# A two-layer decoder on one core: the first attention's norm, projections and value masks in four chunks, GpSimd's turn reordered, one clearing moved

## The reference

```python
def _L0_attn_ref(x, Wq, Wk, Wv, rel_table, gamma, beta):
    q, k, v = (split_heads(x @ W) for W in (Wq, Wk, Wv))   # 16 heads of 8
    attn = softmax(einsum('bhqd,bhkd->bhqk', q, k) * e ** (-0.5))
    bias = rel_table[rel_index].reshape(-1).reshape(h, s, s)
    attn = attn + bias[None]                                # after the softmax
    out = einsum('bhqk,bhkd->bhqd', attn, v)
    out = (out - mu) / sqrt(var + EPS) * gamma + beta
    return out
x = x + _L0_attn_ref(_layernorm(x), ...)
x = x + _L0_xattn_ref(_layernorm(x), ctx_1024, ...)
```

## Time and profile before

| | us |
|---|---|
| time, median of 3 runs | 1696.14 |
| lowest and highest | 1691.09, 1700.21 |
| the profiled execution | 1698.46 |
| its span | 1696.7 |

### The profile page before, as it was taken

How to read it: one execution, slowest core, us unless ns; L and a number is a source line. 1 busy time by engine, 2 the same in 40 slices (tenths; PEclk the granted TensorE clock), 3 DMA queues, 4 the chain that set the end, 5 groups by cost and what they waited for, 6 DMA issues and landing times.

```text
span 1696.7 us, 41331 instructions
## 1 busy us (share of the span) xinstructions
PE 1500.9 (88%) x17052; PEld 956.8 (56%) x17052; DVE 1102.6 (65%) x1846; ACT 868.1 (51%) x1794; POOL 779.0 (46%) x683
## 2 busy tenths in 40 slices
PE   4888999999999788867599999999999999759998
PEld 2556888865444355533366666666666666535554
DVE  5786555532342488868388888888888888515554
ACT  1332333335655333314377777777777777723332
POOL 3665121200000178857477887777777775000000
PEclk9866999989999899977799999999999999969999
DMA  5003000023211230333646556555455455023321
GB/s 114 1 2 102 3 2 3 2 67 99 62 38 24 64 77 1 65 70 73 120 120 127 123 129 129 129 124 127 124 123 129 125 124 115 8 85 76 68 58 22
DMA packets 62458, 129.58 MB, mean 76 GB/s; under 512 B 15709, under 2 KB 37982, under 8 KB 59102
## 3 DMA queue, kind: packets, MB, share of 16 engines
q1 hardware_dynamic: 62270, 126.92, 32.3%
HBM read 100.22 MB, written 26.67 MB: 75 GB/s over the span
## 4 chain that ended last, share of the span: by engine, by line
PE 62%; POOL 13%; DVE 9%; ACT 9%; issue 5%; DMA 2%; SPq 1%; ACTq 0%; DVEq 0%; POOLq 0%
PE ps L831 12%; PE ps L843 9%; POOL ARENA L1879 7%; PE ps L1675 7%; PE ps L1659 4%; POOL ARENA L1885 3%; PE ps L1622 3%; ACT ARENA L1829 3%; PE ps L1613 2%; ACT ARENA L1807 2%; PE ps L520 2%; PE ps L570 2%; PE ps L530 2%; PE ps L1636 2%; PE ps L512 2%
## 5 line engine op out<-in xcount | busy, mean ns | idle before, releaser
L1749 DVE TENSOR_REDUCE ARENA<-ps 112x2 f32<-112x1000 f32 x384 | 456.7, 1198 | 122.3 <-PE ps L1636 119.3
L1829 ACT ACTIVATE ARENA<-ps 125x448 f32<-125x448 f32 x768 | 378.4, 549 | 128.1 <-PE ps L1659 127.1
L1879 POOL TENSOR_TENSOR ARENA<-ARENA 64x500 f32<-64x500 f32 x192 | 266.8, 1390 | 106.8 <-ACT ARENA L1807 88.4
L107 POOL TENSOR_TENSOR rs<-rs,mhalf 128x1 f32<-128x1 f32 x96 | 58.1, 605 | 377.7 <-DVE rs L102 377.5
L831 PE MATMUL ps<-XT,ARENA 128*128 128x448 f32 x544 | 222.4, 553 | 0.0
L1659 PEld LDWEIGHTS ps<-ARENA 64*125 64x125 bf16 x3072 | 122.5, 134 | 134.0 <-ACT ARENA L1829 70.4
L1659 PE MATMUL ps<-ARENA 64*125 64x112 bf16 x3072 | 169.1, 229 | 19.6 <-ACT ARENA L1829 18.5
L1675 PE MATMUL ps<-ARENA 125*17 125x112 f32 x6144 | 185.6, 261 | 0.0
L831 PEld LDWEIGHTS ps<-XT,ARENA 128*128 128x128 f32 x544 | 105.6, 196 | 100.6 <-issue 100.4
L843 PE MATMUL ps<-ARENA 128*128 128x448 f32 x400 | 161.5, 539 | 0.0
L1636 PE MATMUL ps<-ARENA 64*112 64x500 bf16 x768 | 152.8, 387 | 9.0 <-DVE ARENA L1749 8.9
(11 more groups left out here) (228 smaller groups left out, 2205.9 us busy)
## 6 DMA issues: line engine op xcount, KB each, us to landing
ARENA<-key_parts SPq DMA_DIRECT2D x192, 187.5 KB, 4.2
ARENA<-in_ctxT SPq DMA_DIRECT2D x96, 250.0 KB, 3.7
key_parts<-ARENA SPq DMA_DIRECT2D x64, 375.0 KB, 2.8
ARENA<-token_weights SPq DMA_DIRECT2D x32, 512.0 KB, 5.5
ARENA<-in_L_ffn_W SPq DMA_DIRECT2D x1, 2048.0 KB, 9.3
ARENA<-query_parts SPq DMA_DIRECT2D x6, 192.0 KB, 6.9
ARENA<-in_c_ones SPq DMA_DIRECT2D x2, 562.5 KB, 14.3
ARENA<-in_L_attn_a SPq DMA_DIRECT2D x2, 512.0 KB, 5.4
```

The lines of the kernel that those rows point to most:

```text
L1749: e.tensor_reduce(mxp[0:112, b % 2, 2 * g:2 * g + 2, ch], ps[0:112, b1:b1 + 2, 0:500], AX, ALU.max) \
L1829: e.activation(Pb[0:KT, n % NP_, 448 * h:448 * h + 448], ps[0:KT, b1[h], 0:448], ACT.Exp, bias=0.0, scale=1.0).then_inc(exped.sem, 1)
L1879: e.tensor_tensor(T2[r:r + 64, :], T0[64 - r:128 - r, n % 2, :], sin[64 - r:128 - r, sl], ALU.mult) \
```

## The change

- x comes in four chunks of four tiles: GpSimd clears one chunk of `XR` at a time, and SyncE issues that chunk (two transfers each); the identity follows chunk 0.
- The norm of x, the projections and the value masks run chunk by chunk on all four engines: `project(n-1)` and the masks of chunk n-1 stand behind the norm of chunk n. The transposes of the norm use banks 0 and 1 in turn instead of bank 7.
- The transposes of the bias table stand behind the norm of the last chunk, in banks 4 and 5.
- The copies of the keys go from VectorE to ScalarE.
- In the loop `heads(t+2)` stands first in GpSimd's turn. The first masked keys stand ahead of the last pair of doublings.
- The clearing of the cross-attention's `E` goes from ahead of the first attention to turn 16 of its loop.

```diff
         def first_sp(e, w):
             xv = a["x"].rearrange("(t h) s d -> h s t d", h=2)
-            w.wait_ge(*xr_zero(1))
-            for h in range(2):
-                e.dma_start(XR[64 * h:64 * h + S, :, :], xv[h]).then_inc(x_in.sem, 16)
-            e.dma_start(ident[:, :], a["c_ident"]).then_inc(id_in.sem, 16)
+            for n in range(4):
+                sl = slice(4 * n, 4 * n + 4)
+                w.wait_ge(*xr_zero(n + 1))
+                for h in range(2):
+                    e.dma_start(XR[64 * h:64 * h + S, sl, :], xv[h][:, sl]).then_inc(x_in[n].sem, 16)
+                if n == 0:
+                    e.dma_start(ident[:, :], a["c_ident"]).then_inc(id_in.sem, 16)
 
         def first_pool(e, w):
-            e.memset(XR[:, :, :], 0.0).then_inc(xr_zero.sem, 1)
+            for n in range(4):
+                e.memset(XR[:, 4 * n:4 * n + 4, :], 0.0).then_inc(xr_zero.sem, 1)
             e.memset(mhalf[:, :], -0.5).then_inc(half_set.sem, 1)
-            for t in range(NT):
-                ln_power(e, w, 0, t)
...
+                for n in range(5):
+                    if n < 4:
+                        for t in range(4 * n, 4 * n + 4):
+                            final_pe(e, w, 0, t, free, (0, 1))
+                    if n == 3:
+                        w.wait_ge(*rel_in(len(rel_parts)))
+                        for half in range(2):
+                            bk = 4 + half
...
+                    if n:
+                        project(n - 1)
                 scores(0)
...
             def dve(e, w):
+                for n in range(5):
+                    if n < 4:
+                        w.wait_ge(*x_in[n](2))
+                        for t in range(4 * n, 4 * n + 4):
+                            final_dve(e, w, 0, t)
...
+                    if n:
+                        w.wait_ge(*par_in(1))
+                        for v in (2 * n - 2, 2 * n - 1):
+                            w.wait_ge(*v_mm(v + 1))
+                            e.tensor_tensor(Vb[0:112, 4 * v:4 * v + 4, :, 0:16],
...
                 for t in range(NT + 5):
                     v = t - 3
+                    if t + 2 < NT:
+                        heads(t + 2)
                     if 0 <= v < NT:
                         w.wait_ge(*post_eps(v + 1))
                         e.tensor_tensor(rs[:, v:v + 1], rs[:, v:v + 1], mhalf[:, 0:1], ALU.pow).then_inc(post_inv.sem, 1)
                     if 4 <= t < NT + 4:
                         ln_power(e, w, 1, t - 4)
-                    if t + 2 < NT:
-                        heads(t + 2)
+                    if t == NT:
+                        stages[1].parts["prep_pool"](e, w)
...
-                elif k + 1 < 5 and engine != "dve":
+                elif k + 1 < 5 and engine != "dve" and (k or engine != "pool"):
                     stages[k + 1].run("load" if engine == "sp" else "prep_" + engine, e, w)
```

More of the change, by code:

```diff
@@ L92, in decoder @@
         ln_inv, ln_x, ln_t, ln_out = (signal("ln_" + n, 96) for n in ("inv", "x", "t", "out"))
-        xr_zero, half_set = signal("xr_zero", 1), signal("half_set", 1)
-        x_in, id_in = signal("x_in", 2, 16), signal("id_in", 1, 16)
+        xr_zero, half_set = signal("xr_zero", 4), signal("half_set", 1)
+        x_in, id_in = [signal("x_in%d" % n, 2, 16) for n in range(4)], signal("id_in", 1, 16)
         def ln_stats(e, w, k, t):
@@ L251, in scores @@
                     free[b0] = free[b0 + 1] = shifted(t + 1)
[L253 to L260, removed]
@@ L261, in pe @@
-                for n in range(4):
-                    bq, bk = 2 + 2 * (n % 2), 3 + 2 * (n % 2)
-                    sl = slice(512 * n, 512 * n + 512)
[L264 to L282, removed]
+                def project(n):
+                    w.wait_ge(*w_in(3))
+                    w.wait_ge(*ln_out(4 * n + 4))
+                    sl = slice(512 * n, 512 * n + 512)
+                    for bk, wt, mm, cp in ((2 + 2 * (n % 2), wq, q_mm, q_cp), (3 + 2 * (n % 2), wk, k_mm, k_cp)):
+                        if free[bk]:
+                            w.wait_ge(*free[bk])
+                        e.matmul(ps[:, bk, :], wt, xT[:, sl], start=True, stop=True).then_inc(mm.sem, 1)
+                        free[bk] = cp(n + 1)
+                    for v in (2 * n, 2 * n + 1):
+                        bk = 6 + v % 2
+                        w.wait_ge(*doubled(v + 1))
+                        if free[bk]:
+                            w.wait_ge(*free[bk])
+                        for i in range(4):
+                            m = e.matmul(ps[0:112, bk, 128 * i:128 * i + 128],
+                                         xd[:, v % 2, i].rearrange("p f s -> p (f s)"), wv, start=True, stop=True)
+                        m.then_inc(v_mm.sem, 1)
+                        free[bk] = v_cp(v + 1)
@@ new lines, in pe @@
+                for n in range(5):
[6 more added lines that the diff above has]
+                            bk = 4 + half
+                            w.wait_ge(*free[bk])
+                            for i in range(4):
+                                m = e.transpose(ps[0:112, bk, 56 * i:56 * i + 56],
+                                                relb[0:56, 4 * half + i].rearrange("p f k -> p (f k)"), ident[0:56, 0:56])
+                            m.then_inc(rel_t.sem, 1)
+                            free[bk] = bias_cp(half + 1)
+                    if n:
+                        project(n - 1)
@@ L389, in act @@
             def act(e, w):
-                for n in range(4):
-                    w.wait_ge(*q_mm(n + 1))
-                    e.copy(qT[:, 512 * n:512 * n + 512], ps[:, 2 + 2 * (n % 2), :]).then_inc(q_cp.sem, 1)
+                for n in range(5):
+                    if n < 4:
+                        for t in range(4 * n, 4 * n + 4):
+                            final_act(e, w, 0, t, (0, 1))
+                    if n:
+                        m, b0 = n - 1, 2 + 2 * ((n - 1) % 2)
+                        sl = slice(512 * m, 512 * m + 512)
+                        w.wait_ge(*q_mm(n))
+                        e.copy(qT[:, sl], ps[:, b0, :]).then_inc(q_cp.sem, 1)
+                        w.wait_ge(*k_mm(n))
+                        e.copy(kT[:, sl], ps[:, b0 + 1, :]).then_inc(k_cp.sem, 1)
                 for g in range(4):
@@ L420, in heads @@
                                     hm.unsqueeze(1).unsqueeze(3).broadcast_to([128, 2, 8, 56]), ALU.mult).then_inc(heads_p.sem, 1)
+                for n in range(5):
+                    if n < 4:
+                        for t in range(4 * n, 4 * n + 4):
+                            ln_power(e, w, 0, t)
+                    if n:
+                        for v in (2 * n - 2, 2 * n - 1):
+                            w.wait_ge(*ln_out(2 * v + 2))
+                            if v >= 2:
+                                w.wait_ge(*v_mm(v - 1))
+                            e.tensor_copy(xd[:, v % 2], xT[:, 256 * v:256 * v + 256].rearrange("p (b s) -> p b s", b=4)[:, :, 0:56]
+                                          .unsqueeze(2).broadcast_to([128, 4, 2, 56])).then_inc(doubled.sem, 1)
+                    if n == 3:
+                        heads(0)
                 w.wait_ge(*par_in(1))
@@ L424, in pool @@
                               pm[0:112, 0:16:8].unsqueeze(1).broadcast_to([112, B * 8, 2])).then_inc(v_one.sem, 1)
[L425 to L431, removed]
                 heads(1)
@@ L2032, in on_tensor @@
             w = Waits(e)
-            first_pe(e, w)
             program("pe", e, w)
@@ L2037, in on_vector @@
             w = Waits(e)
-            first_dve(e, w)
             program("dve", e, w)
@@ L2042, in on_scalar @@
             w = Waits(e)
-            first_act(e, w)
             program("act", e, w)
@@ L2047, in on_gpsimd @@
             w = Waits(e)
+            first_pool(e, w)
             stages[0].run("prep_pool", e, w)
-            first_pool(e, w)
             program("pool", e, w)
```

36 lines of the change are left out of this document (10 added, 26 removed).

## The result

| | before | changed |
|---|---|---|
| median, us | 1694.04 (4 runs) | 1678.81 (4 runs) |
| lowest and highest | 1691.09, 1700.21 | 1677.89, 1679.51 |
| the profiled execution | 1698.46 | 1677.89 |
| `scores(0)` | 49.20 | 43.53 |
| fifth to sixteenth subtraction (L372) | 67.52 | 55.58 |

The ratio is 0.9898, 95% interval 0.9861 to 0.9934: faster by 1.0%, 15 us between the medians. The prediction was 1687.3 with a range down to 1679, and 1678.81 lies 0.2 under it: the direction was right, the size was not. The profile puts 16.1 us into the first attention alone (151.29 to 135.20). That part wanders by as much on its own, and only the 16.1 are put down to the change.

A forecast was written before the change was run, and what follows sets the result against it. It took the loop to be bound by masked keys in series with VectorE, 6.0 us a turn, after a start with one engine working per phase. -3.0 - 8.1 + 2.3 = -8.8 gave a median of 1687.3, range 1679 to 1697.

The forecast's parts named there:

- the keys' 1.67 stand in series with VectorE: Old loop: masked keys hold VectorE's two-input L355, so their 1.67 us add to VectorE's work in a 6.0 us turn.
- Term two: Loop, fifth to sixteenth subtraction: with heads(t+2) first, 11 turns of 5.4 us take 59.4 instead of 67.5, -8.1 us.
- the term's own end (-12.5): Loop: the fast end of the estimate, turns of VectorE's own 5.0 us, -12.5 us.
- rival 2: Loop: VectorE alone bounds it, turn 5.0, sum -13.2, whole time 1682.9; chance 0.20.
- I take 5.4 per turn: Loop: turn length chosen between 4.96, from the 0.63 mean clock, and TensorE's 6.02 at half clock.
- rival 1: Loop: TensorE's half clock is the bound, turn 6.02, loop -1.3, sum -2.0, whole time 1694.1; chance 0.22.
- Term one: Launch to `scores(0)`: x in chunks brings `scores(0)` to 46.2 instead of 49.2, -3.0 us.
- rival 3: Start: x does not come early, chunk 0 lands at 9, sum -5.3, whole time 1690.8; chance 0.10.
- starts every burst cold: Projections: TensorE working in bursts with waits between falls to the throttled clock each time, which rules out the -7.6 end.
- Term three: Turn 16: clearing the next stage's E delays that stage's norm by +2.3 us, ends 1.7 and 2.9.
- the far end of term one: Up to `scores(0)`: TensorE keeps the full clock through all four projections, `scores(0)` at 41.6, -7.6 us.
- Rival 4: Loop: masked keys collide anew with L355, turn 6.7, loop +5.9, sum +5.2, whole time 1701.3; chance 0.08.

The follow-up runs named there:

- three key buffers: Kernel before with three buffers for the masked keys instead of two, keys still behind both powers: median 1694.77, ratio 1.0000, loop 64.4 us.
- keys first only: Kernel before with one edit, heads(t+2) first in GpSimd's turn: median 1683.24, ratio 0.9951, loop 58.1 us.
- taking both away: Kernel before with three buffers for the masked keys and without the two-input add L355: 1676.60 in one run, loop 54.5 us.
- the added transposes: Changed kernel with the first four of the eight transposes of L301 issued twice in every turn: median 1682.54, ratio 0.9942, loop 56.5 us.
- whole-x run: Changed kernel with x cleared and loaded whole as before, the rest chunk by chunk: median 1684.47, ratio 0.9954, `scores(0)` at 50.5.
- the masks late: Changed kernel with VectorE's value masks of chunk n-1 one chunk later: median 1664.83, ratio 0.9836, `scores(0)` at 30.8.
- the clearing in that gap: Changed kernel with late value masks and the clearing of E behind the first two doublings: median 1666.84, ratio 0.9846, `scores(0)` at 33.9.

## Why the prediction was wrong

**What bounds the kernel.** The step "the keys' 1.67 stand in series with VectorE" was right and is shown (three key buffers: 6.00 a turn; keys first only: 58.1 instead of 67.5). It was not the whole: a second chain of about the same length, late keys to `scores` to L317 to VectorE, bounded turns at the half clock, and only taking both away (54.5) or moving the keys (55.6) opens the loop. The prediction had taken TensorE's 6.0 as a rate. That fits the turn it read, 120.20 to 126.22, in which TensorE never paused; but in 7 of the 11 turns TensorE waited for keys, 10.8 us in all, and the prediction has no term for that.

**Term two, the loop: -8.1 forecast, -11.9 measured.** This is the step that failed. The turn is 5.05, VectorE's own 5.0 of the earlier trace rows, so the term's own end (-12.5) and rival 2 were near. It failed at "I take 5.4 per turn": the granted clock was carried over from the slower loop (0.63, and 0.52 in its last part) as if it were given. In the runs the clock went with the turn: 0.63 to 0.68 where a turn took 5.9 to 6.1 us, 0.75 to 0.84 where it took 5.0 to 5.3, and 0.91 with still more work for TensorE. Seen from TensorE the whole gain is clock: its busy time in the loop falls from 56.0 to 44.6, its idle time stays (11.6, 11.0). That VectorE sets the new turn, and not the clock, is shown by VectorE's missing waits and by the added transposes; why the clock rises with the shorter turn is not shown. The row of 114 to 136 us, from which rival 1 drew its 0.22, was a TensorE that waited for keys in two turns (1.22 and 0.60) and ran the next two without a pause at the half clock.

**Term one, up to `scores(0)`: -3.0 forecast, -5.7 measured.** The order of events was right: VectorE idle 5.1 and 4.8 us ahead of the masks, the bias table behind chunk 3. Sizes were off: chunk 0 landed at 4.2 and not 5.5 (the 4.2 us to landing were read from loads elsewhere in the kernel), and the first two projections took 5.3 and 5.2 us and not 6.1 (11.82 to 17.13, 21.83 to 27.0). The third took 6.4 and not 5.6: it was priced shorter because "the clock has had the longer run", but it ran its queries and keys wholly at half. The whole-x run shows that the start counts in full; rival 3 fell at 4.19. (The change adds six issues on SyncE, not seven, and the scaling of 4.39 is itself the sixteenth; neither enters the sum.)

The "starts every burst cold" drawn from the Trainium skill (TensorE: Matmul & The Clock Gate, section "HAM oscillation — how this bites in real kernels") holds for the queries and keys of the first and third burst. In the seven kernels cut this way the third burst's take 3.78 each time. The second burst's vary: in the changed kernel they began at the full clock, which fell between 22 and 23 us (3.06), in three of the seven they ran wholly at half (3.62). With the masks late there is one burst, and the full clock stays, which agrees with the rule; with the clearing in that gap it fell once more, at 25 us, although TensorE had waited no more than 0.7 us at a time since the burst before.

**Term three, the clearing: +2.3 forecast, +1.5 measured**, below its lower end of 1.7; moved away it gave back 1.2. The Trainium skill's rule (SBUF — State Buffer, section "Who interferes with whom"), that a GpSimd instruction which only writes SBUF does not hold a VectorE instruction with two SBUF inputs, had spoken for 1.75, and the trace agrees: 0.29 for L355 inside the clearing, 1.35 beside the keys, which read SBUF.

**Sum.** -8.8 forecast, -16.1 in the profiles, -15.2 in the medians; of the missing 7.3, 3.8 are term two, 2.7 term one, 0.8 term three. All three missed on the same side, so nothing cancelled. The chances named 0.48 for faster by over 0.5%. The prediction did work out rival 2 together with the far end of term one (1677.7), but left it out of the range as unlikely. That the median fell 0.2 outside the range and not inside is chance; that the loop was priced 3.8 us too long is not.

Rival 4 (a new collision) did not come: L355 was lengthened in 5 of 16 turns, by at most 0.23.

## What to carry to other kernels

When an engine's operation lies on a loop's chain, list every closed chain through it before pricing its removal: two of equal length hide each other, and experiments that cut one at a time gave 3 us each of the 13 that both gave together. Don't carry TensorE's granted clock from a loop that waits into one that doesn't; work out the new turn first, and then ask whether TensorE at the full clock fits. And where work is cut in chunks, keep a consumer's step on the producer's engine one chunk behind: here that step, two value masks ahead of the next chunk's norm, cost more (12.8 us) than the whole of term one won (5.7).

## What the runs showed of the hardware that was not expected

- More work for TensorE, 0.5 us per turn at full clock, went with a mean granted clock of 0.91 instead of 0.81 and left its busy time at 45 us.
- A clearing of 128x3072 on GpSimd left a two-input add on VectorE at 0.29 us; a 128x896 multiply on GpSimd made it 1.35.
- After the first burst the full clock outlasted 4 us of waiting with four transposes of 0.30 us and fell only in the next burst, between 22 and 23 us. In three other kernels with the same bursts it fell within that wait: from the second transpose on they took 0.45.
